# First group's mixing matrix ahead of the bias tables, first expert's transposes inside the shared expert, 16 weight buffers and five widths for 34 experts

## What is computed

```python
def _L0_cond_ref(x, subjects, weights, bias):       # one of 8 mixing matrices over the 32 tokens
    w = weights[subjects]; b = bias[subjects]
    return jnp.einsum('bct,bcd->bdt', x, w) + b[:, :, None]

def _L0_ffn_ref(x, U, V, W1, b1, W2, b2):
    h = jax.nn.relu(jnp.einsum('bsd,de->bse', x, W1) + b1)
    alpha = jax.nn.softmax(jnp.einsum('bse,ek->bsk', h, W2) + b2, axis=-1)
    vx = jnp.einsum('krd,bsd->bskr', V, x)
    uvx = jnp.einsum('kdr,bskr->bskd', U, vx)
    return jnp.einsum('bsk,bskd->bsd', alpha, uvx)

def _L1_cond_ref(x, id, W, b):                      # one of 16 matrices of 256x256 per sequence
    return jnp.einsum('bsi,bio->bso', x, W[id]) + b[id][:, None, :]

def _L1_ffn_ref(hidden_states, ...):                # 64 experts, 6 per token, at most C = 384 rows each
    scores = jax.nn.softmax(x @ gate_w.T, axis=-1)
    topk_w, topk_idx = jax.lax.top_k(scores, TOP_K)
    ...
    g = jnp.einsum('ecd,efd->ecf', buf, w_gate)
    u = jnp.einsum('ecd,efd->ecf', buf, w_up)
    eo = jnp.einsum('ecf,edf->ecd', jax.nn.silu(g) * u, w_down)
    ...
    return y + _shared_swiglu(hidden_states, sh_gate, sh_up, sh_down)
x = x + _L0_ffn_ref(_L0_cond_ref(x, itok_B_0_7, ...), ...)
x = x + _L1_ffn_ref(_L1_cond_ref(x, itok_B_0_15, ...), ...)
```

## Time and profile before

| what | us |
|---|---|
| median of three runs | 540.35 (537.68 to 542.27) |
| the profiled execution, its own time | 540.61 |
| its span from the first to the last instruction | 538.9 |
| TensorE busy | 490.7 (91%) |
| VectorE busy | 297.8 (55%) |
| ScalarE busy | 187.6 (35%) |
| GpSimd busy | 300.3 (56%) |

### The profile page before, as it was taken

How to read it: one execution, slowest core, us unless ns; L and a number is a source line. 1 busy time by engine, 2 the same in 40 slices (tenths; PEclk the granted TensorE clock), 3 DMA queues, 4 the chain that set the end, 5 groups by cost and what they waited for, 6 DMA issues and landing times.

```text
span 538.9 us, 10609 instructions
## 1 busy us (share of the span) xinstructions
PE 490.7 (91%) x2505; PEld 361.4 (67%) x2505; DVE 297.8 (55%) x825; ACT 187.6 (35%) x398; POOL 300.3 (56%) x249
## 2 busy tenths in 40 slices
PE   1979999999999998899999999999899999999940
PEld 1525536464456554778889888888888787989730
DVE  7733856748488213535456555654666455546435
ACT  0121223212130111434455545554555454546300
POOL 4001047777677770247767666566657556768540
PEclk9979999999999999999999999999999999999985
DMA  5865969879734953689899999998999999855389
GB/s 169 272 187 189 368 205 310 277 238 308 248 146 133 357 195 95 180 192 211 201 239 240 232 246 218 262 234 197 254 252 244 236 221 210 198 106 85 37 182 321
DMA packets 88184, 117.17 MB, mean 217 GB/s; under 512 B 14464, under 2 KB 74288, under 8 KB 88112
## 3 DMA queue, kind: packets, MB, share of 16 engines
q1 hardware_dynamic: 55456, 57.05, 34.7%
q0 software_dynamic: 21840, 30.18, 27.2%
q10 hardware_dynamic: 10816, 28.97, 17.2%
HBM read 78.88 MB, written 39.16 MB: 219 GB/s over the span
## 4 chain that ended last, share of the span: by engine, by line
PE 85%; DVE 6%; issue 3%; DMA 3%; ACT 1%; POOLq 0%; SPq 0%; POOL 0%; DVEq 0%; ACTq 0%
PE bank L1133 28%; PE bank L1158 10%; PE bank L1157 10%; PE bank L1064 8%; PE bank L985 6%; PE bank L1101 6%; PE bank L919 4%; PE bank L1077 3%; PE bank L1002 3%; PE bank L931 2%; PE bank L1017 1%; DVE sil L665 1%; PE bank L948 1%; DMA cw<-acc 1%; DMA acc<-OH,sids 1%
## 5 line engine op out<-in xcount | busy, mean ns | idle before, releaser
L513 POOL DMA_INDIRECT acc<-sil,sids x64 | 97.6, 1525 | 68.4 <-ACT sil L612 34.6
L496 POOL DMA_INDIRECT slot_rows<-ctok,sli x96 | 97.4, 1014 | 56.0 <-issue 28.1
L513 POOL DMA_INDIRECT acc<-OH,sids x63 | 96.1, 1526 | 55.3 <-issue 35.6
L882 DVE TENSOR_TENSOR hh<-sg,bank 48x384 f32<-48x384 f32 x64 | 35.6, 556 | 59.7 <-ACT sg L599 48.6
L612 ACT ACTIVATE sil<-bank,wcol 128x256 f32<-128x256 f32 x64 | 29.7, 474 | 52.4 <-PE bank L1158 51.2
L612 ACT ACTIVATE OH<-bank,wcol 128x256 f32<-128x256 f32 x64 | 29.8, 474 | 49.6 <-PE bank L1158 47.8
L597 ACT ACTIVATE sg<-bank 128x384 f32<-128x384 f32 x64 | 31.5, 491 | 36.8 <-PE bank L1133 35.4
L1064 PE MATMUL bank<-cTs,sgus 128*128 128x512 f32 (+1 forms) x96 | 42.2, 593 | 0.5 <-ACT base L544 0.5
L1101 PE MATMUL bank<-ident,cw 128*128 128x128 f32 x276 | 40.7, 273 | 2.0 <-DVE xgT L856 2.0
L1101 PEld LDWEIGHTS bank<-ident,cw 128*128 128x128 f32 x276 | 34.1, 141 | 9.0 <-issue 2.8
L884 DVE TENSOR_TENSOR hh<-sg,bank 128x384 f32<-128x384 f32 x64 | 35.5, 555 | 2.6
(11 more groups left out here) (227 smaller groups left out, 925.8 us busy)
## 6 DMA issues: line engine op xcount, KB each, us to landing
cw<-in_cW SPq DMA_DIRECT2D x64, 256.0 KB, 4.0
cw<-slot_rows SPq DMA_DIRECT2D x94, 136.0 KB
wb<-in_wblk ACTq DMA_DIRECT2D x10, 496.0 KB, 4.1
slot_rows<-blank SPq DMA_DIRECT2D x72, 68.0 KB, 3.6
acc<-zrow POOLq DMA_DIRECT2D x2, 2048.0 KB
cw<-acc SPq DMA_DIRECT2D x8, 512.0 KB, 6.1
bd<-in_wblk ACTq DMA_DIRECT2D x8, 496.0 KB
z<-in_wblk ACTq DMA_DIRECT2D x8, 496.0 KB, 4.2
```

The costliest lines, as they stand in the source:

```text
L496: pool.indirect_dma_start(slots_d, bass.IndirectOffsetOnAxis(sli[:, g % 2, k, t:t + 1], 0), ctok[:, g % 2, t, :], None, bounds_check=SLOTS ...
L513: pool.indirect_dma_start(acc[u % 2], bass.IndirectOffsetOnAxis(sids[0:rows, u % SR, j:j + 1], 0), yo[u % UE][0:rows, j, :], None, bounds_ ...
L882: v.tensor_tensor(hh[0:FT, u % 2, 1, :], sg[0:FT, 1, :], bank[4][CU:CU + FT, 0:CAP], ALU.mult).then_inc(s_hh, 1)
```

## The change

Five things are changed.

- VectorE makes the first group's mixing matrix ahead of the first bias table. TensorE does the four mixing products first and the bias product last in each bank, and waits for the bias table only there.
- VectorE's three remaining pieces move into `group(0)`: the parts of the second bias (`cond_bias`) behind the split of the mixture weights, the one-hot table between the second and the third product `z`, and the large bias table behind the fourth.
- TensorE does the transposes of expert 0 between the last two chunks of the shared expert, and tiles 0 and 1 of the last group's shared down product inside step 0; VectorE's addition of them follows in its step 0. Tiles 2 and 3 stay at the end. Bank 7 takes the place of bank 0 for tiles 0 and 1.
- There are 16 weight buffers for 12; the four new ones lie in the part of `cw` behind the rows.
- The widths are 160, 216, 280 and 384 for 160, 224, 288 and 384, and for 34 experts (e mod 16 below 9, and e above 1) five: 144, 184, 248, 312 and 384.

```diff
-NW = 12
+NW = 16
-WIDTHS = [160, 224, 288, CAP]
+WIDTHS4 = [160, 216, 280, CAP]
+WIDTHS5 = [144, 184, 248, 312, CAP]
...
+        past_rows = cw_flat[:, UE * TJ * RW:]
+        wb += [past_rows[:, i * WROW:(i + 1) * WROW] for i in range(4)]
...
-        SDB = [(7, 6), (0, 1)]
+        SDB = [(7, 6), (7, 0)]
...
+            dve.wait_ge(s_wall, 16 * (BT + 1))
+            mixing(0, TG)
             link(v.tensor_copy(fs3[0:NS0, :], fs_s[:, :]))
...
             biases(0, BG)
-            mixing(0, TG)
             mixed(0)
             mixing(TG, TT)
-            biases(BG, B)
...
-            v.tensor_scalar(ohb[:, :, :], f_b1[:, :].unsqueeze(2).to_broadcast([K3, B, S]), pm[:, 0:1], None, ALU.is_equal)
...
+            def cond_bias():
+                dve.wait_ge(s_w, 16 * 8)
...
                 if g:
                     slots_begun()
+                else:
+                    cond_bias()
                 for c in range(KC):
                     if g and c == 2:
                         slots_summed(g - 1)
+                    elif c == 2:
+                        v.tensor_scalar(ohb[:, :, :], f_b1[:, :].unsqueeze(2).to_broadcast([K3, B, S]), pm[:, 0:1], None, ALU.is_equal).then_inc(s_cb3, 1)
...
+                if g == 0:
+                    biases(BG, B)
...
                 for c in range(DC):
-                    mm(bank[c][:, :], onesb[0:K3, :], bias0[:, g * BG:(g + 1) * BG, :].rearrange("p b s -> p (b s)"),
-                       start=True, stop=False)
...
+                    if g == 0:
+                        pe.wait_ge(s_bias0, 1)
+                    mm(bank[c][:, :], onesb[0:K3, :], bias0[:, g * BG:(g + 1) * BG, :].rearrange("p b s -> p (b s)"),
+                       start=False, stop=True).then_inc(s_mix, 1)
...
-                by_widths(WIDTHS)
+                by_widths(WIDTHS5 if u % 16 < 9 and u > 1 else WIDTHS4)
...
+                if first:
+                    shared_down(G - 1, [0, 1])
...
+                if isinstance(e, int) and e == 0:
+                    pe.wait_ge(s_sb, 2 * (G - 1) + 1)
...
+            for g in range(1, G):
+                shared_chunk(g, 1)
+                if g == G - 1:
+                    pe.wait_ge(s_flags, 2)
+                    pe.wait_ge(s_hs, len(SCH) * g + 1)
+                    pe.sem_inc(s_tick, 1)
+                    tokens(0, 0)
+                shared_chunk(g, 2)
...
-            shared_down(G - 1, [0])
+            shared_down(G - 1, [2])
             down(E - 1, E - 1)
-            shared_down(G - 1, range(1, TG))
+            shared_down(G - 1, [3])
```

59 lines of the change are left out of this document (26 added, 33 removed).

## The result

The changed kernel takes **535.9 us** (median of 19 runs, 533.58 to 540.75). The kernel before took 540.92 beside it (19 runs), so the ratio is **0.9926**, 95% interval 0.9898 to 0.9954. I had predicted 532.6. The time lies inside the range of 528.8 to 537.3, the direction is right, and the gain is half of what I forecast: 4.0 us by the ratio in place of 8.05, and it is not faster by over 1%. The ratio takes in all executions; the two medians alone are 5.0 us apart.

A forecast was written before the change was run, and what follows sets the result against it. TensorE bounds the kernel (85% of the chain), so only its waits and its own work count. Terms -7.35+1.4+1.2-3.3 = -8.05 us, from 540.61 to 532.6 us; range 528.8 to 537.3.

The forecast's parts named there:

- parts 1 to 3: Start of the kernel: matrix first, three VectorE pieces moved, half clock gone; together -7.35 us.
- Part 1: Start: mixing matrix ahead of the bias table, table ready at 11.88, first layer at 16.0; gain 0.63 us.
- Part 2: Group 0: three VectorE pieces moved behind the first softmax end TensorE's 3.53 us pause; TensorE gains 4.16 us there.
- Part 3: Group 0, transposes to conditional layer: half clock behind the pause goes; 3.2 us, bounds 0 and 3.2.
- Rival (b): Start: clock stays low although the pause goes; 532.6+3.2 = 535.8 us, chance 0.10.
- Parts 4 and 5: Before and in step 0: expert 0's transposes inside the shared expert +1.4 us, half the shared down product in step 0 +1.2.
- part 5: Step 0: half of the last group's shared down product added, step takes 6.2 us; +1.2 us.
- at full clock -0.3: Step 0 with the moved shared down product: 4.7 us at full clock against 4.96 before.
- rival (c): Expert start: more weights in flight delay the last scatters, first expert rows later than 199.5; 536.0 us, chance 0.08.
- Part 6: Expert steps: new widths save 488 columns at 10 ns, less slack and third comparisons; -3.3 us, bounds -4.9 and 0.
- Rival (e): 34 expert steps: branches into a larger program stall TensorE, branch rows above 0.5 us; 546.8 us, chance 0.04.
- Part 7: Weight loading: 16 buffers gain nothing, weights being early already; cost 0.

The follow-up runs named there:

- b: Changed kernel with GpSimd's three memsets waiting for the first bias table instead of the mixing matrix; 535.48 us, ratio 0.9926.
- r: Changed kernel with 22 unused identity products on TensorE from 5.2 to 10 us and 6 before the first layer; 639.28 us on a slow chip, ratio 0.9854.
- d: Kernel before with the new widths only; 536.66 us, ratio 0.9927.
- g: Kernel before with only two tiles of the last group's shared down product moved into step 0; 537.96 us, ratio 0.9983.
- c: Kernel before with only the new start: mixing matrix first and three VectorE pieces moved; 536.86 us, ratio 0.9952.
- j: Kernel i with 16 weight buffers in place of 12; 533.07 us, ratio 0.9875.
- l: Kernel i with expert 0's transposes inside the shared expert and their copies ahead of the last chunk's silu and product; 531.79 us, ratio 0.9859.
- i: Kernel before with the new start, new widths and GpSimd's memsets held back, 12 buffers; 532.15 us, ratio 0.9848.
- m: Kernel before with expert 0's transposes inside the shared expert and two shared down tiles in step 0; 541.64 us, ratio 1.0040.
- s_before_busy: Kernel before with 28 unused identity products ahead of TensorE's first wait and 6 before the first layer; 647.15 us on a slow chip, ratio 0.9997.
- q: Kernel l with 22 unused identity products from 5.2 to 10 us and 12 before the first layer; 637.69 us on a slow chip, ratio 0.9838.

## Why the prediction was wrong about the size of the gain

The step that failed is the forecast of the start, parts 1 to 3 at -7.35 us. It took the table chain on VectorE at its old 1.85 us, the first layer at full clock, and the 3.2 us of half clock as something that every execution of before pays. The runs showed 3.78 us for the chain, 5.82 us in place of 3.67 for the first layer's records, no such half clock in two of the five profiles with the old start, and -2.6 us in all. The rest of the sum held within the noise.

**Part 1, wrong in sign.** It took VectorE's table chain as 1.85 us "in another order". It is the same instructions, but moved into the time of GpSimd's memsets, where it takes 3.78 (10.11 to 13.89). Instead of 0.63 gained, 0.92 was lost. b shows that the memsets did 1.2 us of this.

**Part 2, right in mechanism.** The 3.53 us pause is gone. But "TensorE gains 4.16 there" took the first layer at full clock from 16.0 on. Until 21.9 it was not: from first layer to transposes 12.69 us, where the forecast had 10.63 and r with the clock up 10.46. So the gain at the transposes was 0.53 and not 4.16: 1.57 us went with the late start of the first layer, 2.06 with its slow records. The 4.16 already held part 1's 0.63.

**Part 3, the price that did not last.** I wrote "I take 3.2" for the half clock in the one profile of before. There it held: from transposes to conditional layer 11.08 us (30.26 to 41.34) in place of 14.28. But other executions of the old start don't have it (d, g: conditional layer at 42.5 and not 45.1), so the total time can have only a part of it. And I let all that follows move with the start, with no term for a half clock elsewhere; the one at 93.6 us took back 2 us by the third group. Rival (b), "the clock stays low at the start", came in part: what it kept low was the first layer, at 2.1 us and not 3.2. That its 535.8 is near the measured 535.9 is luck. Parts 1 to 3 came out at -3.73 at the first conditional layer of the profile, at -1.66 at the third, and at -2.6 in the total time (c).

**Parts 4 and 5, right in size, part 5 with some luck.** Forecast 1.4 and 1.2, in the profile 18.23-15.36=2.9 together, and 2.8 us between j and b. The "at full clock -0.3" of part 5 was wrong: it set a step at full clock against one with the half clock, and at full clock on both sides it costs 0.9 (g). The forecast that the transposes win nothing was right with its reason, the order of the copies, which l confirms. The sign set for rival (c), rows later than 199.5, came too and says nothing: the last group's chunk 0 was itself 5.7 us later than forecast, and the rows came about as long behind it as before.

**Part 6, right in the total time** (3.9 by d for 3.3, with an interval of 1.9 to 6.0). Step by step: 384 columns to 312 took a step from 6.04 to 5.32, just 72 columns of 10 ns, and the third comparison cost 0.1 us or less, where I had 0.21. Step 7 of width 144 took 3.64, not 3.73. In the profile only 1.3 us are left of it (282.76 to 281.46), since steps 35 to 39 lost 4.9. Rival (e)'s sign, a branch row above 0.5 us, did come (2.47, 0.77 and 0.57 us), but at three branches and not in 34 steps, and its time did not. The Trainium skill (Runtime: NRT & Kernel Launch, Instruction fetch mechanics) says that a taken branch whose target is outside what was read must wait for the fetch. The trace agrees in so far as TensorE's instruction queue starts a read of 16,384 bytes at 385.4, just behind the start of the 2.47 us branch, and the pause became 0.73 us in the one profile with padding. It is not proof: the read takes 1.04 us and ends 1.4 us ahead of the branch, and such reads start every 4 to 12 us in both kernels, most of them without a long branch.

**Part 7, right within the noise:** nothing that can be told (i and j).

**The sum by the measured ratios:** start -2.6 (c), widths -3.9 (d), transposes and down product +2.2 (m) give -4.3, measured -4.0. Each term has an interval of about 2 us to either side, so this shows that no large part is missing, and not more.

Open stay: why the clock falls near 93 us without a pause and only with the new start, what brings the half clock where the experts begin, what decides whether the first layer runs slowly, and which executions meet a long branch.

## What to carry to other kernels

If a kernel's times fall into two clusters, ask which of them the profile shows before you price a pause or a half clock at its full length; the change may only take away the slower one. Read a gain at a later place too: 3.73 us at the first conditional layer were 1.66 at the third. When short VectorE operations move, look at what GpSimd does in the new place and not only at their old durations: here a cast of eight partitions took 1.32 us instead of 0.17. And before you move a piece ahead of a wait, follow its result through the other engines' order to the next wait: with the copies left in place the pause stayed (2.54 us), and with the copies moved another of 1.62 us took its place.

## What the runs showed of the hardware that I had not expected

**GpSimd's memsets hold VectorE's casts but not its two-input operations:** 0.68 and 1.32 us against 0.17 and 0.17, each ending within 0.03 us of a memset's end, while a TENSOR_TENSOR took 0.18 beside one. Two inputs were seen in this one operation only.

**The clock row can say 1.00 where TensorE is slow.** The stretch from 15 to 22 us prints 1.00, but the first layer's eight records took 5.82 us there and 3.60 to 3.67 at full clock. The first record of the clock in that trace begins at 21.9 (in the trace of before at 15.0), and the row has nothing ahead of it; durations tell.

**One chip took 20% longer for every kernel,** the one before too. Two stretches of s_before_busy there (columns as above; granted clock 1.00, then 0.50), and what TensorE did in the second:

```profile
54.90:85.60 30.70, 28.33 (x149) 14.10 (x147) 19.34 (x62) 6.76 (x14) 7.98 (x8) 1.00 0.86 289
85.60:116.30 30.70, 14.97 (x51) 8.54 (x52) 3.18 (x11) 1.14 (x3) 15.72 (x16) 0.50 0.51 162
```

```profile
96.11 0.13 PEld L1008 LDWEIGHTS bank<-cw,x1T 128*32 128x32 f32 x1 [0.60 <-issue]
...
98.20 0.59 PE L1008 MATMUL bank<-cw,x1T 128*32 128x256 f32 x1 [2.19 <-issue]
...
99.60 0.59 PE L1008 MATMUL bank<-cw,x1T 128*32 128x256 f32 x1 [0.81 <-issue]
```

These are the records of the conditional layer, of which 32 take 1.93 us on the other chips. Here they stand 1.4 to 2.8 us apart, and each waits for nothing that the profile shows. In the same execution the first group's 32 records took 1.93 us too. So it is more than half a clock. Four such stretches of 20.5 to 30.7 us lie between 85 and 294 us. A copy on VectorE in the middle of them (0.42 us) was no longer than elsewhere. The cause stays open; the ratios of q and r to the kernel before still came out at 0.984 and 0.985 there.
